# A 512-step recurrence with attention: key scores also laid out with the keys on partitions, candidate and z gates merged, x products taken from DRAM, background work moved to new slots

## The reference, cut to what matters

```python
def step(h, x_t):                     # h: (4, 128), 512 steps, each needs the one before
    proj = h @ W
    score = jnp.einsum('bsh,bh->bs', enc_hiddens, proj)     # 77 keys
    attn = jax.nn.softmax(score, axis=-1)
    context = jnp.einsum('bs,bsh->bh', attn, enc_hiddens)
    inp = jnp.concatenate([x_t, context], axis=-1)
    gx = inp @ kernel + bias
    gh = h @ recurrent_kernel
    xz, xr, xh = (gx[:, :Hd], gx[:, Hd:2 * Hd], gx[:, 2 * Hd:])
    hz, hr, hh = (gh[:, :Hd], gh[:, Hd:2 * Hd], gh[:, 2 * Hd:])
    z = jax.nn.sigmoid(xz + hz)
    r = jax.nn.sigmoid(xr + hr)
    cand = jnp.tanh(xh + r * hh)
    h_new = z * h + (1.0 - z) * cand
    return (h_new, h_new)
```

## Time and profile before

| | |
|---|---|
| median of 3 runs | 3068.23 us (3067.42 to 3076.98) |
| profiled execution, its own time | 3084.98 us |
| its span, first to last instruction | 3082.8 us |
| granted TensorE clock, mean over the span | 0.970 |
| busy over the span: TensorE matmuls, VectorE, ScalarE, GpSimd | 88%, 70%, 56%, 32% |
| matmul instructions | 54163 |

### The profile page before, as it was taken

How to read it: one execution, slowest core, us unless ns; L and a number is a source line. 1 busy time by engine, 2 the same in 40 slices (tenths; PEclk the granted TensorE clock), 3 DMA queues, 4 the chain that set the end, 5 groups by cost and what they waited for, 6 DMA issues and landing times. The chain is left out here.

```text
span 3082.8 us, 131006 instructions
## 1 busy us (share of the span) xinstructions
PE 2726.5 (88%) x54163; PEld 1797.8 (58%) x54163; DVE 2146.9 (70%) x8143; ACT 1713.6 (56%) x5762; POOL 997.4 (32%) x1992
## 2 busy tenths in 40 slices
PE   7999999888778999899999899999989888888769
PEld 4666666575455555565566566666656545444439
DVE  5666666773432888788888688888878766777653
ACT  4666666533443666576776576666657544333322
POOL 2000000231110566355766355555535311000015
PEclk9999999999878999999999999999999999999989
DMA  4000000000011000000001010000001000000013
GB/s 142 5 5 7 5 6 5 11 1 1 19 30 42 7 14 31 4 31 17 11 10 31 4 44 4 11 7 11 28 3 33 8 4 3 4 3 4 3 45 80
DMA packets 41077, 56.47 MB, mean 18 GB/s; under 512 B 6238, under 2 KB 27688, under 8 KB 40360
## 3 DMA queue, kind: packets, MB, share of 16 engines
q1 hardware_dynamic: 36392, 42.46, 4.4%
q0 software_dynamic: 4096, 5.67, 1.0%
HBM read 42.45 MB, written 5.67 MB: 16 GB/s over the span
## 5 line engine op out<-in xcount | busy, mean ns | idle before, releaser
L2183 POOL TENSOR_TENSOR gru_terms<-gru_states,gru_signs 128x8 f32<-128x8 f32 x512 | 104.2, 204 | 1147.5 <-DVE gru_states L2470 1043.5
L2103 ACT ACTIVATE gru_p<-gru_ps_sg,gru_negmax 128x78 f32<-128x78 f32 x512 | 167.6, 327 | 331.1 <-DVE gru_negmax L2439 326.3
L2107 ACT ACTIVATE gru_th_r<-gru_pre_r 128x32 f32<-128x32 f32 x512 | 119.4, 233 | 406.6 <-DVE gru_pre_r L2450 406.6
L1691 PE MATMUL gru_ps_sg<-ctx_gate_w,gru_p_t 128*4 128x64 f32 x12288 | 267.3, 220 | 0.1
L368 ACT ACTIVATE self_probs<-self_sc,self_negmax 128x512 f32<-128x512 f32 x256 | 174.4, 685 | 166.1 <-DVE self_negmax L425 166.1
L2159 POOL TENSOR_SCALAR bg_probs<-bg_probs,bg_arsum 128x256 f32<-128x256 f32 (+2 forms) x192 | 241.0, 1255 | 19.0
L1936 PE MATMUL gru_ps_sg<-score_w,gru_states 128*4 128x78 f32 x4096 | 165.1, 234 | 74.2 <-DVE gru_states L2470 73.0
L2439 DVE TENSOR_REDUCE gru_negmax<-gru_ps_sg 128x1 f32<-128x78 f32 x512 | 121.8, 238 | 146.9 <-PE gru_ps_sg L1936 142.3
L2443 DVE STREAM_TRANSPOSE gru_p_t<-gru_p 128x96 f32<-128x96 f32 x512 | 142.7, 279 | 112.7 <-ACT gru_p L2103 112.5
L1940 PE MATMUL gru_ps_own<-late,gru_states 128*4 128x128 f32 x4096 | 208.4, 276 | 0.0
L1691 PEld LDWEIGHTS gru_ps_sg<-ctx_gate_w,gru_p_t 128*4 128x4 f32 x12288 | 172.2, 86 | 38.3 <-issue 0.3
(11 more groups left out here) (421 smaller groups left out, 7302.4 us busy)
## 6 DMA issues: line engine op xcount, KB each, us to landing
bg_w<-in_moe_w SPq DMA_DIRECT2D x48, 256.0 KB, 3.0
bg_wa<-in_wqkv SPq DMA_DIRECT2D x24, 192.0 KB, 2.3
moe_w<-in_moe_w SPq DMA_DIRECT2D x16, 256.0 KB, 2.9
best_w_sb<-in_ec_w SPq DMA_DIRECT2D x16, 256.0 KB
cross_scratch<-ctab_raw SPq DMA_DIRECT2D x16, 154.0 KB
cross_outs<-cross_scratch POOLq DMA_DIRECT2D x4, 576.0 KB, 6.3
late<-in_late SPq DMA_DIRECT2D x1, 2269.5 KB
self_w_sb<-in_wqkv SPq DMA_DIRECT2D x8, 192.0 KB, 2.3
```

Of the source, the lines that this page charges most:

```text
L1691: last = pe.matmul(bank[32 * c:32 * c + B, 0:hi - lo], p_t[:, 32 * k:32 * k + B], gate_w[:, k, 96 * c + lo:96 * c + hi], start=k == 0, sto ...
L2103: act.activation(p[:, 0:CTX + 1], ps_s[:, 0:CTX + 1], ACT.Exp, bias=negmax[:, 0:1], accum_out=total[:, 0:1])\
```

## The change

Tables and masks. `gate_w` gets two columns of `is_key` behind the r columns of each group (34 columns for r, then 64 for candidate and z). The mask is now for the turned scores. `LATE` is put in another order, so that tables which are spent by then leave room (`spare`) for `x_in` and `x_rows`.

The step:

```diff
 for t in range(S):
-    if t:
-        pe.wait_ge(s_own, t)
-    wait_positive(pe, s_xt, t // P)
-    for c in range(4):
-        pe.matmul(ps_own[32 * c:32 * c + B, 0:96], x_t[:, B * t:B * (t + 1)], x_w[:, c, :], start=True, ...)
-    busy = t and before_scores(t - 1)
-    wait_positive(pe, s_u, t)
-    pe.matmul(ps_s[:, 0:CTX + 1], mask_l, mask_r[:, 0:CTX + 1], start=True, ...)
+    busy = t and after_gates(t - 1)
+    wait_positive(pe, s_own, t)
+    if not from_rows(t):
+        ...
+        for c in range(4):
+            pe.matmul(ps_own[32 * c:32 * c + B, 0:96], x_t[:, B * t:B * (t + 1)], x_w[:, c, :], start=True, ...)
+    wait_positive(pe, s_precz, t)
+    pe.matmul(ps_t, mask_l, mask_r, start=True, stop=False, skip_group_check=True)
     if not busy:
-        wait_positive(pe, s_prez, t)
-        for i in range(6):
-            fill_in(2 * P, ps_tz)
+        for i in range(2):
+            fill_in(2 * P, ps_sr)
     pe.wait_ge(s_h, t + 1)
     for b in range(B):
-        last = pe.matmul(ps_s[32 * b:32 * b + B, 0:CTX + 1], state(t), score_w[:, b, 0:CTX + 1], start=False, ...)
+        last = pe.matmul(ps_s[32 * b:32 * b + 32, :], state(t)[:, b:b + 1].broadcast_to([P, 32]), score_w[:, b, 0:CTX + 1], ...)
     last.then_inc(s_score, 1)
+    for k in range(3):
+        for b in range(B):
+            last = pe.matmul(ps_t[32 * b:32 * b + 32, B * k:B * k + B], score_w[:, b, 32 * k:32 * k + 32], state(t), ...)
+    last.then_inc(s_turnedmm, 1)
     for c in range(4):
-        last = pe.matmul(ps_own[32 * c:32 * c + B, 0:P], state(t), h_w[:, c, :], start=False, ...)
+        last = pe.matmul(ps_own[32 * c:32 * c + B, :], state(t), h_w[:, c, :], start=from_rows(t), ...)
     last.then_inc(s_ownmm, 1)
-    after_own(t)
+    ahead_of_gates(t)
     pe.wait_ge(s_exp, t + 1)
-    for c in range(4):
-        last = pe.matmul(ps_t[32 * c:32 * c + B, 0:2], spread, total[:], start=True, stop=True, ...)
-    last.then_inc(s_total, 1)
-    pe.wait_ge(s_own, t + 1)
-    fill_in(P, ps_own)
-    pe.wait_ge(s_pt, t + 1)
-    gate_products(ps_g, 0, 64).then_inc(s_rcmm, 1)
-    pe.wait_ge(s_rt, t + 1)
-    gate_products(ps_z, 64, 96).then_inc(s_zmm, 1)
+    gate_products(ps_r, 0, GATE_C).then_inc(s_rmm, 1)
+    gate_products(ps_cz, GATE_C, GATE_ALL).then_inc(s_czmm, 1)

 # ScalarE
-    act.activation(p[:, 0:CTX + 1], ps_s[:, 0:CTX + 1], ACT.Exp, bias=negmax[:, 0:1], accum_out=total[:, 0:1])
+    act.wait_ge(s_turnedmm, t + 1)
+    act.activation(p_t[:], ps_t, ACT.Exp, bias=negmax[:, 0:1]).then_inc(s_exp, 1)

 # VectorE
+    after_maximum(t)
     dve.wait_ge(s_ownmm, t + 1)
-    dve.tensor_copy(own[:, 0:256:2], ps_own[:, 0:P]).then_inc(s_own, 1)
-    dve.wait_ge(s_exp, t + 1)
-    dve.transpose(p_t[:], p[:]).then_inc(s_pt, 1)
-    dve.wait_ge(s_total, t + 1)
-    dve.reciprocal(rtotal[:], ps_t[:, 0:1]).then_inc(s_rt, 1)
-    before_gates(t)
+    if from_rows(t):
+        ...
+        dve.tensor_tensor(own[:, 0:256:2], ps_own, x_in[:, k % 2, t % CHUNK, :], ALU.add).then_inc(s_own, 1)
+    else:
+        dve.tensor_copy(own[:, 0:256:2], ps_own).then_inc(s_own, 1)
+    dve.wait_ge(s_rmm, t + 1)
+    dve.reciprocal(rtotal[:], ps_total).then_inc(s_rt, 1)
     ...
-    (pre_r, then the candidate's and z's sums of 32 columns each)
+    (pre_r as before, then)
+    dve.wait_ge(s_czmm, t + 1)
+    dve.scalar_tensor_tensor(out=c_and_z, in0=ps_cz, scalar=rtotal[:, 0:1], in1=own[:, 64:192:2], ...)
```

```diff
+def x_rows_of(g, b, n):                       # TensorE, four times for each 128 steps
+    pe.wait_ge(s_own, BULK[g] + b + 1)
+    wait_positive(pe, s_xt, g)
+    pe.matmul(ps_x[0:P - CHUNK, :], x_t[...][:, b, g * P + CHUNK:(g + 1) * P], x_w..., start=True, stop=True)
+def take_x_rows(g, b, n):                     # ScalarE, in after_candidate
+    act.wait_ge(s_xmm, n + 1)
+    wait_positive(act, s_xout, 16 * n)
+    act.activation(x_rows[0:P - CHUNK, :, 0:96], ps_x[0:P - CHUNK, :]..., ACT.Copy)
+def store_rows(g, b, n):                      # SyncE
+    sp.wait_ge(s_xrow, n + 1)
+    sp.dma_start(x_products[g * P + CHUNK:(g + 1) * P, b, :], x_rows...)
+def load_rows(k):                             # SyncE, for every 8 steps, one group of 8 ahead
+    sp.wait_ge(s_xout, 16 * B * (k * CHUNK // P + 1))
+    sp.wait_ge(s_own, (k - 1) * CHUNK)
+    for b in range(B):
+        sp.dma_start(x_in[b:P:32, k % 2, :, :], x_products[k * CHUNK:(k + 1) * CHUNK, b, :]...)
```

```diff
-STAGES = {2: {"project": 0, "squares": 1, "scales": 1, "rows": 2, "turn": 2, "scores": 3, "max0": 4, "exp0": 4, "max1": 5, "exp1": 5,
-              "scale0": 5, "scale1": 6, "probs0": 6, "probs1": 7, "values": 8, "out": 9, "add": 10},
+STAGES = {2: {"project": 0, "squares": 0, "take_v": 1, "sums": 1, "rows": 2, "turn": 2, "take_qk": 2, "scores": 3,
+              "max0": 4, "exp0": 4, "scale0": 4, "max1": 5, "exp1": 5, "scale1": 5, "probs0": 5, "turned0": 5, "probs1": 6, "turned1": 6,
+              "values": 6, "take_out": 7, "out": 7, "add": 8},
...
+ahead_of_gates:  TensorE: one down product; PACE 3: turn, out; PACE 2: probs1
+after_gates:     TensorE: x rows, up, three down products, norms, project, probs0, scores, out, values, turn, gating
+after_exp:       ScalarE: square of a chunk; take_qk (PACE 3); exp0, exp1; turned1, take_out (PACE 2)
+after_candidate: ScalarE: x rows, unit_input, tangent (now at stage 1), squares, take_v, take_qk (PACE 2), turned0
+before_maximum:  VectorE: add_expert, first half of hidden, max0, max1
+after_maximum:   VectorE: second half of hidden, sums, rows, add_out (PACE 2)
+GpSimd:          argument (now at stage 1), norms of q and k, then scale0, scale1
```

More of the change, by code:

```diff
@@ L31 @@
 HEAD = 1
+GATE_C, GATE_ALL = 34, 98
 GELU_LINEAR = (2 / math.pi) ** 0.5
@@ L1568, in recurrence @@
         PACE = {1: 2, 2: 2, 3: 3}
+        STAGES = {2: {"project": 0, "squares": 0, "take_v": 1, "sums": 1, "rows": 2, "turn": 2, "take_qk": 2, "scores": 3,
+                      "max0": 4, "exp0": 4, "scale0": 4, "max1": 5, "exp1": 5, "scale1": 5, "probs0": 5, "turned0": 5, "probs1": 6, "turned1": 6,
+                      "values": 6, "take_out": 7, "out": 7, "add": 8},
+                  3: {"project": 0, "squares": 0, "take_v": 1, "sums": 1, "rows": 2, "turn": 4, "take_qk": 4, "scores": 4,
+                      "max0": 5, "exp0": 5, "scale0": 5, "max1": 6, "exp1": 6, "scale1": 6, "probs0": 6, "turned0": 6, "probs1": 8, "turned1": 8,
+                      "values": 11, "take_out": 11, "out": 12, "add": 13}}
         ATTENTION, GATING, EXPERTS = {1: 0}, {}, {}
@@ new lines, in ahead_of_gates @@
+            def ahead_of_gates(t):
+                for g, n, m in chunks_at(t, 4):
+                    down(g, n, m, range(1))
+                for g, n, m in units_at(t, "turn"):
+                    if PACE[g] == 3:
+                        turn_qk(g, n, m)
+                for g, n, m in units_at(t, "out"):
+                    if PACE[g] == 3:
+                        project_out(g, n, m)
+                for g, n, m in units_at(t, "probs1"):
+                    if PACE[g] == 2:
+                        turn_probs(g, n, m, 1)
@@ L1859, in after_own, with after_gates @@
+            def after_gates(t):
                 busy = False
[L1860 to L1861 removed]
+                for g, b, n in bulk_at(t):
+                    x_rows_of(g, b, n)
                     busy = True
[L1863 to L1869 removed]
@@ L1884, in before_scores @@
                     busy = True
[L1885 to L1898 removed]
+                for g, n, m in chunks_at(t, 4):
+                    down(g, n, m, range(1, B))
                     busy = True
@@ L1903, in before_scores @@
                         busy = True
+                for g, n, m in units_at(t, "project"):
+                    project(g, n, m)
+                    busy = True
+                for g, n, m in units_at(t, "probs0"):
+                    turn_probs(g, n, m, 0)
+                    busy = True
+                for g, n, m in units_at(t, "probs1"):
+                    if PACE[g] == 3:
+                        turn_probs(g, n, m, 1)
+                        busy = True
+                for g, n, m in units_at(t, "scores"):
+                    scores(g, n, m)
+                    busy = True
+                for g, n, m in units_at(t, "out"):
+                    if PACE[g] == 2:
+                        project_out(g, n, m)
+                        busy = True
+                for g, n, m in units_at(t, "values"):
+                    values(g, n, m)
+                    busy = True
+                for g, n, m in units_at(t, "turn"):
+                    if PACE[g] == 2:
+                        turn_qk(g, n, m)
+                        busy = True
                 for at, g in gating_at(t, 5):
```

386 lines of the change are left out of this document (199 added, 187 removed).

## The result

| | before | after |
|---|---|---|
| median, same chip | 3075.03 us (6 runs) | 3088.72 us (6 runs, 3084.79 to 3099.87) |
| ratio, 95% interval | | 1.0055 [1.0035, 1.0075] |
| profiled execution, its own time | 3084.98 us | 3085.65 us |
| recurrence, first state to last | 1964.6 us | 1970.0 us |
| granted clock, mean | 0.970 | 0.883 |

The kernel got slower by about half a percent. The forecast was 2910 us, in a range of 2845 to 3010, with 0.85 on faster. The page of the profile after shows it first in two places: the span and busy time, then TensorE's busy tenths over the granted clock in 40 slices of 77 us, then one row of the costliest groups (its columns are busy us, mean ns of one, idle time before it).

The account below looks back on a forecast made before the run. The 512-step state recurrence was taken as the bound: 1664 us of bare steps plus background, bulk, stalls, setup and clock made 1806 against 1964.6, 158 less; 2927 like the profile, less 16.8, gave 2910 us, range 2845 to 3010.

Parts of the forecast that it names:

- tile 2, excess: Tile 2's attention, 64 steps: turned probabilities ahead of the gates make steps 3.7 us, excess 0.45 each, 29 us.
- tile 1, excess: Tile 1's attention, same chain as tile 2 with 256 columns and shorter scaling: excess 0.13 a step, 8 us.
- tile 3, excess: Tile 3, 96 steps: maxima of 512 columns ahead of the step's own maximum, 0.1 each, 10 us.
- bulk steps, stalls, setup: 16 steps with bulk x products 10 us, stalls once per stage and in first steps 15, setup 4.
- The bare chain: Recurrence step without background: 3.69 us falls to 3.25, with 0.52 gained from turned scores and 0.02 and 0.06 lost.
- rival C: New turned products load one after the other, exponential 0.36 us later every step: 3090 us, slower; chance 0.05.
- Experts (96 steps): Experts' stage: loop from exponential through square, polynomial and product to tanh takes 3.45 to 3.5 us; excess 0.22, 21 us.
- rival B: Heavier: unseen collisions, above all in tile 2, add 0.2 to 0.3 us in 288 background steps: 2945 to 3010; chance 0.20.
- The clock: Two fills per bare step: a good half of some 170 steps at 1.2 GHz, 0.42 each: 45 us, ends 0 and 75.
- nothing on the path: Merged candidate and z sum starts 0.17 us behind pre_r, lasts 0.28, ends before tanh of r returns: no cost.
- Rival D: Clock does not come back, 1.2 GHz in background steps too: 215 us instead of 45, 3150 or more; chance 0.10.
- x products: nothing: Removing four x products per step gains nothing, since TensorE idles there in a bare step.

Follow-up runs that it names:

- e1: Kernel after the change with six fills instead of two in a step without background: 3010.41 us, ratio 0.9768.
- e5: Kernel after with six fills and the c_in scan's tanh of r moved into PSUM (results not the kernel's): 2928.96 us, ratio 0.9522.
- e2: Kernel after with GpSimd's argument and ScalarE's tanh one step later, as in the kernel before: 3056.49 us, ratio 0.9911.
- e6: Kernel after with six fills, argument and tanh one step later, and that tanh ahead of the unit's input on ScalarE: 2928.20 us, ratio 0.9526.
- e9: e6 with the x products in every step, as before the change, and no bulk products: 2970.32 us, ratio 0.9660.
- e12: e10 with the second turned probabilities moved between the r products and the candidate's and z's: 2944.75 us, ratio 0.9569.
- e10: e6 with the scan's factors also in PSUM and the fills ahead of the mask product: 2919.72 us, ratio 0.9498.
- e11: e6 with four fills instead of six in a bare step: 2927.34 us, ratio 0.9527.

## Why the prediction was wrong, point by point

The forecast's recurrence was 1806 us; 1970 were measured. The terms, worked out from the starts of the state scan after and from a bare step of 3.295 us:

| term | forecast | measured after |
|---|---|---|
| 512 bare steps at full clock | 1664 (3.25 each) | 1687 (3.295) |
| experts, excess | 21 | 109 (101 steps of 4.37 in the mean), 87 of it the c_in scan's extra length |
| tile 2, excess | 29 | 41 |
| tile 1, excess | 8 | 17 |
| tile 3, excess | 10 | 24 |
| clock | 45 | 79 (the recurrence of after less that of e1) |
| bulk steps, stalls, setup | 29 | 13 (what is left over) |
| sum | 1806 | 1970 |

The miss of the whole time is 179 us. The recurrence is 164 of it. Of the rest, 20 come from the step from profile to median, which took 16.8 us off where after's own is 3 above its profiled execution, and the parts outside the recurrence gave 5 back.

- **The bare chain: right.** The exponential to the r products took 0.32 us (0.26 forecast, the exponential itself 0.27 and not 0.21), those to pre_r 0.65 as forecast, and the turned products ended at 2782.53, 0.75 us after the state (0.83 forecast), ahead of the exponential. In this step at full clock VectorE's maximum released it, not TensorE. In the bare steps after, at 1.2 GHz, TensorE did, the sign that I had set for rival C; but it cost 0.04 us a step and not 0.36, and the 24 products took 0.35 us together. Rival C, loads in a row, is refuted.
- **The step that failed: "Experts (96 steps)".** It put square, polynomial, product and tanh into one loop on ScalarE and GpSimd and asked only whether that loop is short enough. It is. What it did not ask is what VectorE does meanwhile. The product of 1.28 us, moved by the change from 1.39 us behind the state to 2.52, beside the c_in scan, held the scan by 1.08 us (median) in 81 of 96 steps. The scans are 87 us longer by it, and no term of the sum had it; rival B spoke of collisions not seen, and named others. e1 and e5 show the cause (same overlap, input in PSUM, this scan not held), e2 and e6 the cure by order. What freeing it gives is less than 87: 69 us in e5, where the state scan is held in its place, and 81 us of recurrence in e6 beside e1.
- **"The clock": the mechanism right, the size wrong.** I took 0.42 a step from the kernel before and half of 170 steps. It was every bare step from step 416 on, and many of the 46 ahead of it, at 0.61: 79 us (70 of them behind step 370), over my upper end of 75. The 0.42 was the old chain's; the new one puts 24 products for candidate and z behind r's, and at 1.2 GHz the merged sum is late for the scan, 0.28 us of the 0.61. The working had "nothing on the path" for that sum, which is so at full clock alone. And "after each drop the clock came back within two steps" came from steps that had eight fills again; the new kernel never has. Rival D was half true, in the bare stages and not beyond: the background stages stood at 0.96 to 0.99.
- **"x products: nothing": wrong, in the change's favour.** TensorE idles there in a bare step, as stated, but not in a background step (e9: 42 us, net of the bulk). It didn't spoil the sum, since the excesses were worked out without them. The loads come in 60 groups of 4, not 56; VectorE's `own` was never released by a DMA.
- **Tile 2** came to 3.88 us against 3.7, and for the most part not by the forecast cause. Beside a bare step of 3.30, the longer step of a pair (4.06) loses 0.28 us ahead of the scores, where TensorE is late, 0.22 to the turned probabilities ahead of the gates (r products 0.54 behind the exponential, not 0.32) and 0.27 to the held c_in scan; the shorter one (3.51) loses 0.21 ahead of the scores. The forecast had only the 0.22, which is 7 of 41 us. Moving the turned probabilities behind r (e12) or freeing the scan (e10) didn't shorten the pair; whether less TensorE work ahead of the scores would help was not run. An order with the turned probabilities behind all gates was not tried either: it needs one more step per unit between values and sum.
- Without the two faults (e6, e11) the kernel takes 2928 us, within the range and 18 us over the forecast. That it is so near is luck in part: the forecast has 45 us for a low clock that they don't pay, so the other terms were some 50 us too small.

## What to carry to other kernels

When work is moved to another place in a schedule, lay it beside what every other engine runs at that moment, not only in line with its own chain: a VectorE operation with two SBUF inputs that starts 30 ns after a long GpSimd operation ends with it, however short it is, and one input in PSUM or a start 60 ns earlier makes it free. Then look at the next such operation: freed by PSUM, the first scan handed the hold on to the second. Work that fills an idle TensorE is a term of its own: before it is cut, price every step at the lower clock by the new chain, since there a product that hides at full speed may not.
